# Layer 3 of a graph network: the weighed rows as float32r rounding and remainder, one 264-column product per tile

## The reference

```
h = (x @ W).reshape(N, H, C)
a_src = jnp.sum(h * att_src, axis=-1)
a_dst = jnp.sum(h * att_dst, axis=-1)
logits = a_src[src] + a_dst[dst]
logits = jnp.where(logits > 0, logits, NEG_SLOPE * logits)
seg_max = jax.ops.segment_max(logits, dst, num_segments=N)
e = jnp.exp(logits - seg_max[dst])
denom = jax.ops.segment_sum(e, dst, num_segments=N)
alpha = e / (denom[dst] + EPS)
msgs = h[src] * alpha[:, :, None]
out = jax.ops.segment_sum(msgs, dst, num_segments=N)
...
out = (out - mu) * jax.lax.rsqrt(var + 1e-05) * gamma + beta
return jax.nn.relu(out)
```

## Time and profile before

| | us |
|---|---|
| median of three runs | 6288.9 (6285.21 to 6297.36) |
| profiled execution, span from first to last instruction | 6290.0 |
| layer 3 gathers run in it | 3854.1 to 6222.0 |

### The profile page before, as it was taken

The page is one execution under the profiler, slowest core; times in us unless marked ns, Lnnn a source line. Parts: engine busy times, 40 slices in busy tenths (PEclk is TensorE's granted clock), DMA queues, the critical chain, the costliest instruction groups (busy, mean ns, idle before and its releaser), DMA issues.

```text
span 6290.0 us, 72860 instructions
## 1 busy us (share of the span) xinstructions
PE 4549.5 (72%) x24017; PEld 3664.1 (58%) x24017; DVE 2674.4 (43%) x9938; ACT 1822.6 (29%) x3934; POOL 3113.1 (49%) x3324
## 2 busy tenths in 40 slices
PE   6999978888888898888989995344444444544445
PEld 5888855666666566666669994234444343434334
DVE  8999943333333333333335442233333333333334
ACT  5888842222222222222224552011111111111112
POOL 0000036666666666666640004666666666666663
PEclk9999989999999999999999997666666666666667
DMA  6777765555555555555647784122222222222221
GB/s 152 166 163 167 164 162 178 178 179 177 180 176 179 179 177 179 179 179 177 182 133 220 244 243 112 44 48 48 47 47 48 49 48 47 47 50 48 48 48 29
DMA packets 473053, 804.93 MB, mean 128 GB/s; under 512 B 73183, under 2 KB 301706, under 8 KB 462698
## 3 DMA queue, kind: packets, MB, share of 16 engines
q0 software_dynamic: 140192, 443.73, 28.3%
q1 hardware_dynamic: 318378, 346.76, 18.1%
q10 hardware_dynamic: 14112, 9.74, 0.5%
HBM read 663.72 MB, written 136.22 MB: 127 GB/s over the span
## 4 chain that ended last, share of the span: by engine, by line
PE 47%; another core or an unknown queue 25%; DVE 12%; issue 11%; DMA 2%; ACT 2%; POOL 1%; DVEq 0%; ACTq 0%
PE bank L1034 12%; PE bank L1021 10%; PE bank L1205 7%; PE bank L689 5%; PE bank L669 3%; PE bank L1523 2%; DVE ring L987 2%; DVE ring L1415 2%; DMA atab<-at 2%; PE bank L1487 1%; PE bank L590 1%; POOL ring L550 1%; DVE hs L638 1%; PE bank L970 1%
## 5 line engine op out<-in xcount | busy, mean ns | idle before, releaser
L550 POOL DMA_INDIRECT ring<-ptab,src x1612 | 1526.9, 947 | 854.7 <-issue 446.2
L550 POOL DMA_INDIRECT ring<-htab,src x1612 | 1526.5, 947 | 853.1 <-issue 448.3
L1034 PE MATMUL bank<-ring,oh 128*126 128x384 f32 x3224 | 1257.8, 506 | 30.8 <-issue 30.3
L987 DVE TENSOR_TENSOR ring<-bank,ring 128x512 f32<-128x512 f32 x806 | 543.0, 687 | 1613.4 <-remote 855.2
L1021 PE MATMUL bank<-w1e,ea 128*128 128x256 f32 x3224 | 892.4, 400 | 252.2 <-DVE ring L987 190.9
L1021 PEld LDWEIGHTS bank<-w1e,ea 128*128 128x128 f32 x3224 | 620.1, 199 | 541.1 <-issue 270.9
L1523 PE MATMUL bank<-ring,oh 128*126 128x132 f32 x3224 | 675.6, 357 | 337.0 <-DVE ring L1415 224.6
L1003 ACT ACTIVATE ring<-ring 128x1024 f32<-128x1024 f32 x403 | 425.6, 1056 | 1400.5 <-DVE ring L987 1112.6
L1523 PEld LDWEIGHTS bank<-ring,oh 128*126 128x126 f32 x3224 | 583.5, 252 | 424.0 <-issue 219.9
L1034 PEld LDWEIGHTS bank<-ring,oh 128*126 128x126 f32 x3224 | 624.7, 196 | 290.5 <-issue 74.8
L689 PE MATMUL bank<-xhl,at 128*126 128x258 f32 x3822 | 712.6, 323 | 0.0
(11 more groups left out here) (268 smaller groups left out, 4727.0 us busy)
## 6 DMA issues: line engine op xcount, KB each, us to landing
atab<-at POOLq DMA_DIRECT2D x78, 1543.5 KB, 9.9
ring<-ea_r SPq DMA_DIRECT2D x403, 256.0 KB
ea<-ea_t SPq DMA_DIRECT2D x403, 256.0 KB
adjb<-atab SPq DMA_DIRECT2D x156, 535.5 KB, 4.6
adjb<-atab SPq DMA_DIRECT2D x78, 472.5 KB, 4.5
ring<-ptab,src POOLq DMA_INDIRECT x1612
ring<-htab,src POOLq DMA_INDIRECT x1612
ptab<-pO ACTq DMA_DIRECT2D x49, 128.0 KB, 7.3
```

The lines of the kernel that those rows point to most:

```text
L550: return e.indirect_dma_start(o, None, table, bass.IndirectOffsetOnAxis(ap=src[:, t:t + 1], axis=0))
L987: e.tensor_tensor(group1(gi, m % 2), MLP[m % 3][:, :].rearrange("p (g f) -> p g f", g=2), group1(gi, m % 2), ALU.add).then_inc(s_edge, 1)
L1034: w = e.matmul(SUM[s % 2][0:SL, 0:384], slots_of(s, i), rv1[:, t // G % NR1, t % G, :], start=i == 0, stop=t == END[s])
```

## The change

The rows are weighed as before, now at every second place (k = 0, 2, ... 12). Then each chunk of 3 tiles is split: ScalarE writes it rounded to float32r into a new buffer `split3` (7 chunks, 264 columns for each tile), and VectorE writes the rest, the row less its rounding, beside it. TensorE multiplies `oh`, which is now a float32r tile, with all 264 columns in one float32r product for each tile, four places later than before (`LAG3`). The sums thus stand in two halves, which ScalarE (scaled copy of the second half) and VectorE (`both_halves`, adds the scaled first half) put together. A gather now waits for VectorE's remainder of the chunk in its ring slots (`s_rest`) and no longer for TensorE's products. `slot_hots` moves from k=0 to k=17, and waits for the sums of a group further back. The product for the blocks (`x`, `oh2f`) moves from k=4 to k=8. The ring of layer 1 gets a tensor of its own, in the same amount; its work is the same.

```diff
-                        if s >= NR3 and i % G == 0:
-                            e.wait_ge(s_sum3, START[s - NR3] + min(i + G, SIZE[s - NR3]))
+                        if s >= NR3 and i % CH == 0:
+                            e.wait_ge(s_rest, min(CW[s - NR3] + i // CH + 1, CW[s - NR3 + 1]))
...
-                    slot_hots(e, s, s_oh3, s_sum3)
...
+                elif k == 17:
+                    slot_hots(e, s, s_oh3, s_sum3, CW[s - 1] if s >= 2 else 0)
...
+            def both_halves(e, c):
+
+                e.wait_ge(s_kept3, 2 * c + 2)
+                for i in range(2):
+                    o = odd_from(c) + i
+                    r3 = x2[0:SL, c % 4, i, 0:HROW]
+                    e.scalar_tensor_tensor(out=r3, in0=SUM[c % 2][0:SL, 0:HROW], scalar=par[0:SL, o:o + 1], in1=r3, op0=ALU.mult,
+                                           op1=ALU.add).then_inc(s_both3, 1)
...
-                        if 0 <= g < NS and k % CH == 0 and k < SIZE[g]:
...
+                        if 0 <= g < NS and k % 2 == 0 and CH * (k // 2) < SIZE[g]:
...
+                        if 0 <= g < NS and k and k % 2 == 0 and CH * (k // 2 - 1) < SIZE[g]:
+                            n, q = chunk(g, CH * (k // 2 - 1))
+                            w = rows3(g, CH * (k // 2 - 1), q.shape[1])
+                            e.wait_ge(s_high, n + 1)
+                            e.tensor_tensor(q[:, :, HROW:2 * HROW], w, q[:, :, 0:HROW].bitcast(F32), ALU.subtract).then_inc(
+                                s_rest, 1)
+                        if 0 <= c < NS and k == LAG3 + 2:
+                            both_halves(e, c)
...
+                        if 0 <= g < NS and k % 2 == 1 and CH * (k // 2) < SIZE[g]:
+                            n, q = chunk(g, CH * (k // 2))
+                            e.wait_ge(s_weigh, n + 1)
+                            if n >= NH3:
+                                e.wait_ge(s_sum3, n - NH3 + 1)
+                            e.activation(q[:, :, 0:HROW], rows3(g, CH * (k // 2), q.shape[1]), ACT.Copy).then_inc(s_high, 1)
+                        if 0 <= c < NS and k == LAG3 + 1:
+                            e.wait_ge(s_sum3, CW[c + 1])
...
-                            m = e.matmul(SUM[g % 2][0:SL, 0:HROW], slots_of(g, k), rv3[:, g % NR3 * GT + k, :], start=k == 0,
-                                         stop=k == SIZE[g] - 1)
-                            if k % G == G - 1 or k == SIZE[g] - 1:
-                                m.then_inc(s_sum3, k % G + 1)
+                        g, i = divmod(GT * (u - 2) + k - LAG3, GT)
+                        if 0 <= g < NS and i < SIZE[g]:
+                            n, q = chunk(g, i // CH * CH)
+                            if i % CH == 0:
+                                e.wait_ge(s_rest, n + 1)
+                            if i == 0:
+                                e.wait_ge(s_oh3, g + 1)
+                                if g >= 2:
+                                    e.wait_ge(s_both3, 2 * (g - 1))
+                            m = e.matmul(SUM[g % 2][0:SL, 0:2 * HROW], slots_r(g, i), q[:, i % CH, :], start=i == 0,
+                                         stop=i == SIZE[g] - 1)
+                            if i % CH == CH - 1 or i == SIZE[g] - 1:
+                                m.then_inc(s_sum3, 1)
```

More of the change, by code:

```diff
@@ L117, in build @@
     NR3 = 4
-    RING = max(NR3 * GT * HROW, NR1 * G * 384)
+    CH = 3
+    NH3 = 7
     NEA = 5
@@ L216, in build @@
         xhl = sb("xhl", [P, NB, YW], FR, c=halves0)
-        at0 = sb("at0", [P, 2, NB * SL], FR, c=halves0)
-        halves0.close()
-        ring = sb("ring", [P, RING], c=gathering)
-        oh = sb("oh", [P, 2, GT * (SL + S)], c=gathering)
         bank = [ctx.enter_context(nc.psum_tensor(f"bank{i}", [P, 512], F32)) for i in range(8)]
@@ L229, in slots_of, with slots_r @@
         def slots_of(s, i):
+            return ohf[:, s % 2, SL * i:SL * i + SL]
+        def slots_r(s, i):
             return oh[:, s % 2, SL * i:SL * i + SL]
@@ L470, in build @@
         pre.close()
+        at0 = sb("at0", [P, 2, NB * SL], FR, c=halves0)
+        halves0.close()
+        oh = sb("oh", [P, 2, GT * (SL + S)], FR, c=gathering)
+        ohf = oh[:, :, :].bitcast(F32)
         strays = nc.values_load(flagi[0:1, 0:1], min_val=0, max_val=5 * P)
@@ L528, in expected @@
             halves2.close()
-            def view(n, w):
-                return ring[:, 0:n * G * w].rearrange("p (n g f) -> p n g f", n=n, g=G)
-            rv1 = view(NR1, 384)
             hbf = hflat.bitcast(BF)
@@ L538, in expected @@
             AT = tuple(at0[:, i, :].rearrange("p (b c) -> p b c", c=SL) for i in range(2))
-            rv3 = ring[:, 0:NR3 * GT * HROW].rearrange("p (t f) -> p t f", f=HROW)
             def landed1(gi):
@@ L1212, in tensor2 @@
                         tensor_post2(e, b, k)
-            W3 = weave(GT * (NS + 8), {GT * (s + 3) + 5: bs for s, bs in LASTS.items()}, 24)
+            LAG3 = CH + 1
+            W3 = weave(GT * (NS + 8), {GT * (s + 3) + LAG3 + 6: bs for s, bs in LASTS.items()}, 24)
             V3, A3 = 31, 3
             TOP3, LOG3 = 9, 3
-            CH = 3
             s_hots, s_pack, s_ohT, s_turn, s_rT, s_spread, s_o2, s_o2T, s_dst, s_top, s_most, s_logit_in, s_logit, s_exp, \
-                s_weigh = (sem(f"s_{n}") for n in ("hots", "pack", "ohT", "turn", "rT", "spread", "o2", "o2T", "dst", "top",
-                                                   "most", "logit_in", "logit", "exp", "weigh"))
+                s_weigh, s_high, s_rest = (sem(f"s_{n}") for n in (
+                    "hots", "pack", "ohT", "turn", "rT", "spread", "o2", "o2T", "dst", "top", "most", "logit_in", "logit", "exp",
+                    "weigh", "high", "rest"))
             CW = [sum(-(-n // CH) for n in SIZE[0:s]) for s in range(NS + 1)]
@@ L1228, in odd_from, with rows3, chunk @@
                 return START[s] % 2
-            def rows3(s, n):
-                o = s % NR3 * GT
+            def rows3(s, i, n):
+                o = s % NR3 * GT + i
                 return rv3[:, o:o + n, :]
+            def chunk(g, k):
+                n = CW[g] + k // CH
+                return n, split3[:, n % NH3, 0:min(CH, SIZE[g] - k), :]
             def weights3(o, n):
@@ L1423, in scalar3 @@
                 for u in range(NS + 8):
-                    f, c = u - 1, u - 3
+                    f, g, c = u - 1, u - 2, u - 3
                     for k in range(GT):
-                        if 0 <= c < NS and k == 0:
-                            e.wait_ge(s_sum3, END[c] + 1)
+                        if 0 <= g < NS and k % 2 == 1 and CH * (k // 2) < SIZE[g]:
[6 more added lines that the diff above has]
+                            e.wait_ge(s_sum3, CW[c + 1])
                             if c >= 4:
@@ L1508, in tensor3 @@
                                      start=True, stop=True).then_inc(s_logit_in, 1)
-                        if 0 <= c < NS and k == 4:
-                            e.wait_ge(s_kept3, 2 * c + 2)
+                        if 0 <= c < NS and k == LAG3 + 4:
+                            e.wait_ge(s_both3, 2 * c + 2)
                             e.wait_ge(s_most, 2 * c + 2)
@@ L1538, in any_order @@
             D.sem_inc(s_tick, 16)
+            ring = sb("ring", [P, 2320])
             one = Serial(s_tick, s_own, s_idle)
```

40 lines of the change are left out of this document (20 added, 20 removed).

## The result

The changed kernel takes 6320.16 us in the median of four runs (6316.1 to 6322.47), the kernel before 6293.13 us on the same chip: a ratio of 1.0043 [1.0028, 1.0057], slower by 0.4%. The forecast was 1.5% faster.

A forecast was written before the change was run, and what follows sets the result against it. Layer 3 was taken as bound by a loop: GpSimd streams gathers, TensorE's signals come late, slots stay taken, GpSimd stops. 6290.0 - 106 (layer 3) + 9 (tail) = 6193 us profiled, 6192 by the median; range 6100 to 6270.

The forecast's parts named there:

- sum from a chain: Layer 3, each group: 30.36 us plus 4.4 minus 3.66 gives 31.1, with all hidden 28.0; 29.0 taken, -106 us in all.
- The slots: Layer 3 ring slots, freed by VectorE's punctual remainder at k=14, not k=20: chain not shorter, ring some 6 tiles longer.
- The fifth hand-over: Layer 3: `oh` and the copy `x` no longer wait right behind a group's last product; gain up to 3.66 us each group.
- What VectorE and ScalarE signal isn't late: Layer 3: only TensorE's signals arrive late while gathers stream; TensorE begins L1487 just behind ScalarE's copies.
- Rival B: Layer 3 keeps its pace, since gathers need a share of stopped time; only the tail moves: 6298 us, chance 0.17.
- Rival A: Layer 3: one long gather stream, then a stop of 5.3 us each group (sign: 5 and over); slower, 6356 us, chance 0.25.
- the stops' 250 us: Sign in the profile after: GpSimd's layer 3 gathers wait some 250 us beyond issue, not 354.
- the sign of B: Layer 3 keeps its 2368 us though the waits changed place; the prediction is then wrong.
- TensorE was no bound: TensorE in layer 3: its change costed at nothing; up to 1.5 us each group if the clock fell to 0.5.
- The tail: After the gathers: closing work opens 5 places later and the four last groups carry more, +9 us in all.
- VectorE's additional work is hidden: VectorE in layer 3: 4.4 us more work each group, of which 3.1 us can hide in waits.
- Layer 1 gave nothing: Layer 1 keeps its work, its waits and its ring: no change in time.

The follow-up runs named there:

- b_fifth: Kernel before with `oh` at k=17, `x` at k=5, the block product at k=8, the closing work 4 places later: 6232.71 us, ratio 0.9894.
- a_sumfree: Changed kernel, but a gather waits again for TensorE's products and not for VectorE's remainder: 6246.92 us, ratio 0.9935 to the kernel before.
- b_hop: Kernel before, layer 3 cut to gathers and output writes, plus 3000 signal rounds between VectorE and ScalarE: a round takes 0.36 us, later 1.40.
- b_alone: Kernel before with layer 3 cut down to its gathers and output writes, each gather waiting only for an earlier group's landing: 6126.9 us.
- a_restlate: Changed kernel, but a gather waits for the remainder two chunks behind the one in its slots: 6286.3 us, ratio 0.9971 to the kernel before.
- b_manysig: Kernel before with each layer-3 product raising the semaphore by 1, where every fourth raised it by 4: 5536.26 us, ratio 0.9999, without stops.
- a_rest1: Changed kernel with VectorE's remainder cut to 4 of 132 columns for each tile: 6304.04 us, ratio 1.0028 to the kernel before.
- after_2: Changed kernel run again unedited, where GpSimd never stops: 5571.74 us, ratio 1.0069 to the kernel before.

## Why the prediction was wrong

**The step that failed** is the sum from a chain: it took each wait at its worth and "The slots" at nothing. It had a group go from 30.36 to 29.0 us; it went to 30.65 (2390.5 / 78). Two of its terms show it.

*The fifth hand-over* was mis-sized: up to 3.66 us for each group by the time that `oh` waited, 0.8 us by b_fifth. I took a wait for its worth. Where signals come late, a wait that is taken out turns up at others: VectorE and ScalarE stood idle as long as before, within 25 us each.

*The slots* were costed at nothing, for "They come free by VectorE's remainder, whose signals aren't late". Freed by the remainder they cost 68 us more than freed by the products (a_sumfree), 0.9 us for each group. The signal from VectorE to GpSimd is indeed punctual, 0.27 us. What is late is the remainder, since VectorE waits for late signals ahead of it. "What VectorE and ScalarE signal isn't late" was wrong where it mattered: b_hop shows ScalarE's signal to VectorE 1.04 us late with TensorE idle, and the trace after shows VectorE 3.01 us late for its own. I had read punctual signals from one place, inside a stop of GpSimd.

Why signals are late stays open.

**Rival B** came nearest, at 0.17, and is right in part. Its "share of stopped time that the gathers need" is what b_alone shows, a pace of 1.40 us whatever is waited for, 212 of the 351 us. It gave 6298 us; with the 27 us by which the gathers got longer it would have given 6325. That the stops' sum stayed (351, then 347 us) is partly luck, though: everything but who frees the ring took it to 274, and the ring's release brought it back. B had the change move nothing but the tail, while b_fifth and a_sumfree moved the time by 65 and 44 us. What I held against it, that a stop ends with a signal and not after a fixed time, was no argument: the signal is what is late. The other hint stood in the earlier trace rows, two layers of different work with the same length. But the share isn't fixed: 318 us in b_fifth, 274 in a_sumfree.

**Rival A** has a part of it: fewer and longer stops (4.3 us on average, 2.8 before), and a gain from freeing slots later (a_restlate). It isn't the whole, since the sum of the stops didn't grow, and with 347 / 78 = 4.4 us of stop for each group its own sign, 5 us, wasn't reached. Whether the number of semaphore increments counts where signals are late was not tested: b_manysig, with 21 instead of 6 for each group, ran only where nothing is late.

**The length of a gather** stood nowhere in the sum: 27 us, 0.35 for each group. It is the loss that is there with the stops and without them.

**What held.** Of the signs that were given, the stops' 250 us failed, and the layer kept its length, which was named as the sign of B. VectorE's remainders are 0.56 us each; its work in layer 3 is 1020 us (forecast 1110), ScalarE's 546 (600). TensorE was no bound, at a granted clock of 0.55 instead of 0.65. The tail grew by 8.4 us (9). That VectorE's additional work is hidden held too, as a_rest1's stops and after_2 show. Layer 1 gave nothing.

**By parts**, where GpSimd stops: everything of the change but who frees the ring, -44 us (a_sumfree, in which the longer gathers are already paid), the ring freed by the remainder, +68 us: +24 us, measured +27. This is a way to split the result and no check of it, since the 68 us are the difference of the two kernels.

## What to carry to other kernels

Before a long chain of waits is costed, look for what all of them have in common: if two stages of different work run at one pace, take out a wait and it comes back at the next one, and the worth of an edit is what a kernel with that edit alone shows. A resource that is freed earlier is no gain when its user is already the one that runs ahead; where GpSimd stops, later slots, or a pause in the stream, were faster. A vector operation beside a stream of indirect gathers can lengthen those that overlap it (944 to 1011 ns here), and that loss doesn't depend on who waits for whom. And a time that differs by 12% between two sets of runs of one program is to be looked into before an edit is judged by 1%.

## What the runs showed of the hardware

In the first half of the runs (up to b_hop) a stream of 128-row indirect gathers, started each 1.25 us, falls to one each 1.40 us after 188 of them (b_alone; 174 in b_hop), where a gather itself takes 1.10 us instead of 0.94. The data and the writes to the semaphore are there after 2.2 to 2.4 us all the same, and SyncE goes on 3.3 us after the last start. From the 16th gather on, a hand-over from ScalarE to VectorE takes 1.11 us instead of 0.07, until 27 us after the last gather; the one from VectorE to ScalarE takes 0.03 us throughout, and the one from VectorE to GpSimd 0.27.

In the second half nothing of this is seen in 1612 gathers. The same program takes 6290 us in the first and 5537 us in the second. Chip number 0 stands in both halves, and the traces of the first hold little over a third of the updates of semaphores that those of the second hold. Whether the chip, its state or the recording makes the difference no run here shows.

In both halves gathers that overlap the 128x396 remainder, 0.56 us on VectorE, get longer: the mean of 1612 goes from 947 to 964 ns, and to 954 or 955 with the remainder cut to 4 of 132 columns.
